# Feed-forward weights turned over in earlier halves, and the low part of x ahead of the pair's statistics, in a one-core transformer-like block on Trainium2

## What is computed

```
x = x + attention(layernorm(x))      # gated linear attention with a delta rule, state 128 x 128
x = x + ffn(layernorm(x))            # h = silu(x Wg) * (x Wu);  h Wd;  width 384
x = x + state_space(layernorm(x))    # convolution, 4 heads of 64, chunked scan, gate, RMS norm
x = x + ffn(layernorm(x))            # the same weights again
```

## Time and profile before

| | us |
|---|---|
| median of 3 runs (857.46 to 860.45) | 860.03 |
| the profiled execution | 861.55 |
| its span, first to last instruction | 859.7 |
| PE busy in the span | 774.4 (90%) |
| PE weight loads | 552.5 (64%) |
| VectorE (DVE) busy | 614.7 (72%) |
| ScalarE (ACT) busy | 536.2 (62%) |
| GpSimd (POOL) busy | 561.8 (65%) |

### The profile page before, as it was taken

How to read it: one execution, slowest core, us unless ns; L and a number is a source line. 1 busy time by engine, 2 the same in 40 slices (tenths; PEclk the granted TensorE clock), 3 DMA queues, 4 the chain that set the end, 5 groups by cost and what they waited for, 6 DMA issues and landing times. The chain is left out here.

```text
span 859.7 us, 15957 instructions
## 1 busy us (share of the span) xinstructions
PE 774.4 (90%) x5114; PEld 552.5 (64%) x5114; DVE 614.7 (72%) x1739; ACT 536.2 (62%) x1035; POOL 561.8 (65%) x917
## 2 busy tenths in 40 slices
PE   3599999999999877999848899999999999959997
PEld 3478888888888764666625466655655555636665
DVE  3568778878878436888583778988878776638885
ACT  3234444345444243888545788888897887719886
POOL 1567667767766504878610798779768866747885
PEclk9979999999999886999756999999999999979999
DMA  4341221121111000000000000000000000000112
GB/s 122 96 121 38 61 67 30 28 56 29 29 42 43 14 1 1 0 1 0 2 3 6 1 1 7 4 1 1 9 2 1 8 2 2 1 1 25 50 50 75
DMA packets 59420, 22.16 MB, mean 26 GB/s; under 512 B 22224, under 2 KB 59088, under 8 KB 59344
## 3 DMA queue, kind: packets, MB, share of 16 engines
q1 hardware_dynamic: 59344, 21.23, 9.6%
HBM read 11.59 MB, written 9.63 MB: 25 GB/s over the span
## 5 line engine op out<-in xcount | busy, mean ns | idle before, releaser
L1429 DVE SCALAR_TENSOR_TENSOR arena<-bank,convw_sb,arena 128x510 f32<-128x510 f32 (+2 forms) x192 | 142.5, 745 | 42.1 <-ACT arena L918 37.5
L687 POOL TENSOR_TENSOR arena<-arena 128x768 f32<-128x768 f32 x64 | 114.9, 1816 | 10.5 <-ACT arena L945 10.5
L661 POOL TENSOR_TENSOR arena<-ff,arena 128x512 f16<-128x512 f32 x64 | 73.6, 1160 | 23.7 <-ACT arena L887 21.7
L882 ACT ACTIVATE ff<-bank 128x512 f32<-128x512 f32 x96 | 56.3, 586 | 36.7 <-PE bank L1732 36.5
L592 POOL TENSOR_TENSOR leafV<-leafV,leaf_tmp 32x14 f32<-32x14 f32 (+6 forms) x224 | 62.4, 278 | 17.5
L1819 PE MATMUL bank<-xnT,win_sb 128*128 128x512 f32 x128 | 71.8, 644 | 0.0
L1245 DVE SCALAR_TENSOR_TENSOR ff<-bank,ff 128x512 f32<-128x512 f32 x96 | 64.7, 685 | 9.7 <-ACT ff L882 9.0
L790 ACT ACTIVATE ff<-bank 128x256 f32<-128x256 f32 (+2 forms) x80 | 34.0, 425 | 57.4 <-PE bank L1571 36.1
L939 ACT ACTIVATE arena<-bank 128x384 f32<-128x384 f32 x128 | 59.9, 492 | 13.6 <-PE bank L1834 13.5
L783 ACT ACTIVATE xn<-x_all,shift,rstd 128x128 f32<-128x128 f32 x136 | 55.6, 480 | 20.2 <-DVE shift L1048 20.1
L588 POOL TENSOR_TENSOR leaf_tmp<-leafV 32x14 f32<-32x14 f32 (+6 forms) x224 | 56.6, 253 | 16.4
(11 more groups left out here) (202 smaller groups left out, 2241.8 us busy)
## 6 DMA issues: line engine op xcount, KB each, us to landing
LT_dram<-arena SPq DMA_DIRECT2D x16, 256.0 KB, 2.3
ff<-R_dram SPq DMA_DIRECT2D x16, 256.0 KB, 2.9
out<-x_all SPq DMA_DIRECT2D x8, 512.0 KB, 3.2
x_all<-in_L_attn_a_x SPq DMA_DIRECT2D x7, 512.0 KB, 5.5
ff<-pieces_dram SPq DMA_DIRECT2D x48, 6.0 KB
x_all<-in_L_attn_a_x SPq DMA_DIRECT2D x2, 256.0 KB, 4.0
R_dram<-tab SPq DMA_DIRECT2D x2, 256.0 KB, 7.2
leafV<-LT_dram SPq DMA_DIRECT2D x16, 32.0 KB, 1.9
```

What stands on the lines that cost most here:

```text
L661: nc.gpsimd.tensor_tensor(of_block(hl[u], j), hidT[u][:, j, :], of_block(hh[u], j), ALU.subtract).then_inc(hl_done[u], 1)
L687: nc.gpsimd.tensor_tensor(score[h], cb[g % 2], hgam[h], ALU.mult).then_inc(score_done, 1)
L882: nc.scalar.activation(silu_g[u][:, j, :], bank[u][(1, 3, 1)[j]][:, :], ACT.Silu, scale=DEQUANT).then_inc(silu_done[u], 1)
L1429: nc.vector.scalar_tensor_tensor(acc_of[:, :, s:SEQ], src_of[:, :, 0:SEQ - s], convw_sb[:, r, TAPS - 1 - s:TAPS - s], acc_of[:, :, s:SEQ], ...
```

## The change

In attention, the nine weight transposes and six copies leave the opening of half 18. `gate` and `up` are turned in `ahead` of half 16 on PE, into `begin_bank[0]` and `[1]`, and copied out in `ahead` of half 17 on ACT, float32 and float16 one after the other. `down` is turned in `ahead` of half 18 into `begin_bank[0]`, once the four copies are out, and its two copies stand behind the copy of w0. `widest` is turned into `begin_bank[1]`. PE's wait for the last g goes. In both feed-forwards, `low_x(0, 0)` moves ahead of the two `pair_stats(1, u)`.

```diff
+            def weights_out(n, turned, wide, narrow16):
+                act.wait_ge(ffT_mm, n + 1)
+                for dst in (wide, narrow16):
+                    nc.scalar.activation(dst, turned[:, 0:HIDDEN], ACT.Copy).then_inc(ffT_done, 1)
...
                     copy_out(w0tok[k % 2], end_bank[0][:, 0:BATCHES * P], w0_mm, n, w0_done)
+                    if n == GROUPS - 1:
+                        weights_out(2, begin_bank[0], downT[:, :, :].rearrange("p k d -> p (k d)"), down16[:, :])
...
-                if h == GROUPS + LAG_END - 1:
-                    for n, dst in enumerate((gateT[:, :], upT[:, :], downT[:, :, :].rearrange("p k d -> p (k d)"))):
-                        act.wait_ge(ffT_mm, n + 1)
-                        nc.scalar.activation(dst, begin_bank[n][:, 0:HIDDEN], ACT.Copy).then_inc(ffT_done, 1)
-                    for n, dst in enumerate((gate16[:, :], up16[:, :], down16[:, :])):
-                        nc.scalar.activation(dst, begin_bank[n][:, 0:HIDDEN], ACT.Copy).then_inc(ffT_done, 1)
+                if h == GROUPS + 1:
+                    weights_out(0, begin_bank[0], gateT[:, :], gate16[:, :])
+                    weights_out(1, begin_bank[1], upT[:, :], up16[:, :])
...
-                    nc.vector.tensor_reduce(widest_all[:, :], inv_bank[0][:, 0:P], AX.X, ALU.max).then_inc(widest_step, 1)
+                    nc.vector.tensor_reduce(widest_all[:, :], begin_bank[1][:, 0:P], AX.X, ALU.max).then_inc(widest_step, 1)
...
+                low_x(0, 0)
                 for u in U:
                     pair_stats(1, u)
-                low_x(0, 0)
...
+            def weights_turned(n, to):
+                for k in range(FF_BLOCKS):
+                    last = nc.tensor.transpose(to[:, cols(k)], ff_raw[:, n, cols(k)], ident)
+                last.then_inc(ffT_mm, 1)
...
+                if h == GROUPS:
+                    pe.wait_ge(ff_float, 1)
+                    pe.wait_ge(LTraw_done, done(GROUPS - 1))
+                    weights_turned(0, begin_bank[0])
+                    weights_turned(1, begin_bank[1])
                 if h == GROUPS + LAG_END - 1:
-                    pe.wait_ge(ff_float, 1)
-                    pe.wait_ge(g_done, done(GROUPS - 1))
-                    for n in range(3):
-                        for k in range(FF_BLOCKS):
-                            last = nc.tensor.transpose(begin_bank[n][:, cols(k)], ff_raw[:, n, cols(k)], ident)
-                        last.then_inc(ffT_mm, 1)
+                    pe.wait_ge(ffT_done, 4)
+                    weights_turned(2, begin_bank[0])
                     pe.wait_ge(widest_step, 3)
-                    nc.tensor.transpose(inv_bank[0][:, 0:P], widest[:, 0:1].broadcast_to([P, P]), ident).then_inc(widest_mm, 1)
+                    nc.tensor.transpose(begin_bank[1][:, 0:P], widest[:, 0:1].broadcast_to([P, P]), ident).then_inc(widest_mm, 1)
```

## The result

The changed kernel takes **852.97 us** (median of 7 runs, 851.75 to 857.49), the kernel before 858.9 beside it (7 runs, 857.41 to 864.6): a ratio of 0.9932 with a 95% interval of 0.9906 to 0.9957. In a second comparison (12 and 29 runs) it was 855.02 against 858.49, 0.9951 [0.9927, 0.9975]. Over the runs of all comparisons the means are 859.56 (107 runs, standard error 0.28) and 854.58 (19 runs, 0.50): a gain of about 5.0 us, 0.6%, with an error of 0.6. Executions more than 1.5% above the fastest of their kernel are left out of all means (two of before, both at 870 us, none of the change).

A forecast was written before the change was run, and what follows sets the result against it. Taken to bound the kernel: half 18's link-by-link chain, with transposes and copies on its path, and PE's clock. 1.84 - 0.5 + 1.4 + 0.9 = 3.6 us gave a median of 856.4, range 853.2 to 859.3.

The forecast's parts named there:

- Start of half 18: Last attention half: fewer transposes before w0 and its copy ahead of the `down` copies bring the correction 1.84 us earlier.
- Half 17: Four weight copies at the head of ACT's half 17 delay w0's copy and the correction: loss 0.5 us, between 0 and 0.7.
- Half 16: Six transposes (0.67 us) ahead of w0 cost nothing, covered by PE's later 2.92 us wait for the inverse's transpose on DVE.
- Clock in half 18: Last attention half: PE's clock falls only behind L1645 (PT), gaining 1.4 us; bounds 0 and 3.65.
- Low part of x first: Start of both feed-forwards: xl ahead of the statistics gains 0.5 and 0.7 us, taken as 0.9 after rounding.
- Rival E: Feed-forward starts: PE idles about 1.5 us for POOL, keeping the clock low longer; 5.6 us lost, 862.0; chance 0.04.
- rival B: Half 18: no clock fall before x is stored, 5.9 us gained in all, 854.1; chance 0.26.

The follow-up runs named there:

- the swap alone: The kernel before with only `low_x(0, 0)` moved ahead of the two `pair_stats(1, u)`: 858.24 us, ratio 0.9992; on another chip 855.85, 0.9967.
- the fourth trace of after: The changed kernel, unaltered, traced in one more single execution that is in no mean: span 849.5 us.

## Why the prediction was right and wrong

The forecast was 856.4, the range 853.2 to 859.3. The measured 852.97 lies 0.2 under the range; the second comparison's 855.02, with 12 runs instead of 7, lies inside, and the mean gain of 5.0 us stands against the 3.6 of the sum. So part of the miss is the luck of seven executions.

- *Start of half 18*: forecast 1.84, measured 1.90 (14.22 to 12.32). Right, with the wait of "some 0.6" at 0.47.
- *Half 17*: forecast a loss of 0.5, measured 0.43. Right; ACT's copy slipped by 0.58 us against the store of group 13's x (298.70 - 296.06 to 298.65 - 295.43), the v products covered part of that, and the correction's wait was 0.17 and not 0.5.
- *Half 16*: costed at nothing. Right, but not only by the cover that was named. The six transposes took 0.71 us (275.83 to 276.54) and first filled a wait of 0.47 us ahead of half 16's w0, which is gone; the rest went into the later wait for DVE, now 2.84 or 2.85 us against 2.92. That wait ends 6.86 us behind the store of group 12's x in both profiled traces.
- *Clock in half 18*: **the step that failed.** The term took the fall of the earlier trace rows as what this kernel does, and asked only at which link it would come after the change. Three more traces of before have no fall in half 18. The bound of 3.65 for "no fall until x is stored" was exact: 17.88 - 14.22 = 3.66. After the change half 18 ran at 1.00 in all four traces, where the term had a fall behind L1645. Against the profiled execution the clock gave 3.65 us and not 1.4. Against the runs it is a price paid in one execution of several, so what the change could save of it on average is at most that price times a chance that I had no row for: with 1 in 6, 0.6 us. The sum's own time hid this: the profiled execution carried a fall that the other traces of before didn't.
- *Low part of x first*: forecast 0.5 and 0.7 (1.2 together, of which the sum took 0.9). With the low stretch over in time the traces give 0.5 in the first feed-forward (87.7 to 87.2) and, in three of four, 1.1 to 1.3 in the second (the mean of four traces before is 88.53; after 87.42, 87.40, 87.28). This term was too small: L1547 stood 7.89 us behind in the profiled trace, but 8.18 in the three others of before. In L1551's distance from `xl` or x stored: 7.42 where 7.7 was forecast and 8.18 stood, and 7.22 where the forecast was 7.2. The first product came 1.7 us earlier and not 2.4, since the register load and branch that the prediction left open are on the path: it starts 1.38 us behind the start of `xl`, where it had stood 3.09 behind the store of x (331.94 - 328.85), and 0.74 with the load ahead.
- *Rival E* got a chance of 0.04 for a net loss. No net loss came, but a low stretch over the work behind PE's wait cost 2.3 and 2.1 us in the first feed-forward in two of four traces of after (89.49, 89.32), and once in the second (89.69). In one of the two in the first it began in the wait, as E has it, in the other ahead of it. My argument against E, that the transposes come no later than before, was true and did not bear on where the low stretch lies.

Correcting the failed term does not bring the sum to the measured gain. With 0.6 for the clock and the measured 1.90, 0.43 and 1.7 for the other three it is 3.8. Of the 5.0 us, the path in halves 17 and 18 explains 1.5, and the swap alone was measured at 2.1 with an error of 0.6. The rest, about 1.4 us with an error near 1, is not placed; a rarer fall in half 18 could be part of it. In the four traces of each kernel, half 18's fall adds 0.9 to the mean of before, and 0.7 lies ahead of group 13's store, where the fourth trace of after had no low stretch in half 16; four traces are too few to call either the change's doing. What stays open too is why the grant falls where it does. The Trainium skill, TensorE: Matmul & The Clock Gate (What's actually happening), says that the clock's monitor runs freely and isn't restarted with the kernel; the traces agree, since the same program had its falls at different links in different executions, and the same instructions of half 18 ran in 14.22 us and in 17.88. Part 4 of that page (PE-mode transpose), by which a transpose doesn't count as busy time in the same way, is neither borne out nor refuted: the waits filled with transposes kept a grant of 1.00, but so did five in six traces of the old opening with its waits left empty.

The range failed in its width: its lower end was set from rival B "less part of the runs' own spread", with three times of before in a band of 3.0 us. Twenty-nine runs of before span 10 us (854.90 to 864.91), and the two medians of the change lie 2 us apart.

## What to carry to other kernels

A path that waits link by link, at one clock, can be priced from rows to a tenth of a us, even across a reordering, as in halves 17 and 18. A clock fall in one trace can't: before a term is made of it, ask for a second trace of the same kernel, and price it as a chance times a cost. And where a change lets PE start earlier, look at the next thing that it must wait for: here the statistics were the real head of the chain, and moving them into idle time in the layer before, with the flag loaded earlier, gave as much again as the whole change.

## What was unexpected of the hardware

The low level comes and goes between executions of one program on one chip, at 1.3 to 4 us a fall, and the times of this kernel spread over 10 us (854.90 to 864.91 in 29 runs). Half 16's fall near 282 us came behind or in PE's wait of 2.8 to 2.9 us in 16 of the 18 traces, and not in the other two, with the same wait; there x of group 13 was stored 2 to 4 us sooner (292.80 and 292.09 against 294.5 to 296.4). With the statistics taken out of the hand-over, two of three traces had no low stretch between 290 and 411 us, where every trace of the change had one within 10 us of the store of x.
